# Gated graph layers: GRU tile updates spread over successive steps, and 10 instead of 12 of every 26 edge quads summed densely

## The reference

```
h = relu(layernorm(x)) @ lin_w.T + lin_b
for i in range(3):
    m = h @ weight[i]
    agg = segment_sum(m[src], dst, num_segments=12500)
    h = gru_cell(agg, h, w_ih, w_hh, b_ih, b_hh)
return x + h
# gru_cell: r = sigmoid(ir + hr); z = sigmoid(iz + hz)
#           n = tanh(inn + r * hn); h = (1 - z) * n + z * h
```

## Time and profile before

| what | value |
|---|---|
| median of 3 runs | 5887.51 us (5881.04 to 5918.47) |
| the profiled execution's own time | 5864.06 us |
| its span, first to last instruction | 5862.2 us |
| granted TensorE clock over the span | 0.787 of full speed |
| busy: PE / DVE / ACT / POOL | 65% / 31% / 19% / 59% |
| moved by DMA | 992.59 MB, 169 GB/s |

### The profile page before, as it was taken

One profiled execution on the slowest core, in us unless ns is written; L12 is line 12 of the kernel. 1 busy time (PEld: TensorE's weight loads), 2 busy tenths in 40 slices (PEclk: granted clock), 3 DMA queues, 4 the chain that ended last, 5 costly groups with the idle time before them and its releaser, 6 DMA issues.

```text
span 5862.2 us, 83667 instructions
## 1 busy us (share of the span) xinstructions
PE 3831.5 (65%) x31796; PEld 2541.3 (43%) x31797; DVE 1824.9 (31%) x7602; ACT 1102.4 (19%) x2163; POOL 3481.9 (59%) x3518
## 2 busy tenths in 40 slices
PE   4255555544455554444358888888875888888887
PEld 3144444433344444333224444544542444444454
DVE  7233434433333443333212222222221222222222
ACT  3133333333333333332100000000010000000000
POOL 5766555666665565665556566565645655656554
PEclk8566666766666666666679999999987999999998
DMA  5545444544445454444546666666664666666664
GB/s 181 153 128 141 139 136 138 148 128 130 135 131 143 140 146 126 137 135 118 171 150 213 204 204 212 209 206 204 217 211 150 211 202 200 210 206 199 204 214 140
DMA packets 726236, 992.59 MB, mean 169 GB/s; under 512 B 74424, under 2 KB 606520, under 8 KB 725816
## 3 DMA queue, kind: packets, MB, share of 16 engines
q1 hardware_dynamic: 471336, 582.73, 30.8%
q0 software_dynamic: 165888, 339.96, 21.2%
q10 hardware_dynamic: 88592, 64.25, 3.6%
HBM read 755.57 MB, written 231.08 MB: 168 GB/s over the span
## 4 chain that ended last, share of the span: by engine, by line
PE 52%; another core or an unknown queue 20%; issue 15%; ACT 5%; DVE 5%; DMA 1%; DVEq 1%; POOL 0%; ACTq 0%; POOLq 0%; SPq 0%
PE psum L758 26%; PE psum L738 9%; PE psum L736 4%; ACT pieces_region L591 4%; PE psum L716 4%; PE psum L704 3%; PE psum L675 1%; PE psum L676 1%; PE psum L677 1%; DVE onehot L1036 1%; DVE pieces_region L1137 1%; PE psum L688 1%; DVE aggT L1073 1%; DVEq L1026 1%
## 5 line engine op out<-in xcount | busy, mean ns | idle before, releaser
L468 POOL DMA_INDIRECT ring_region<-messages,edge_src x3456 | 3421.4, 990 | 2268.5 <-issue 1003.1
L758 PE MATMUL psum<-stage_region,pieces_region 128*128 128x432 f16 x9408 | 1862.7, 353 | 163.4 <-issue 161.6
L738 PE MATMUL psum<-pieces_region,stage_region 128*128 128x112 bf16 (+1 forms) x5376 | 998.4, 268 | 1160.3 <-ACT pieces_region L591 568.8
L758 PEld LDWEIGHTS psum<-stage_region,pieces_region 128*128 128x128 bf16 x9408 | 911.6, 99 | 1039.4 <-issue 317.2
L738 PEld LDWEIGHTS psum<-pieces_region,stage_region 128*128 128x128 bf16 x5376 | 641.0, 121 | 1345.2 <-issue 1266.0
L591 ACT CAST pieces_region<-psum 128x504 f16<-128x504 f32 x1344 | 759.5, 580 | 1830.8 <-remote 1005.8
L1059 DVE TENSOR_TENSOR aggT<-aggT,psum 128x36 f32 x864 | 166.7, 193 | 2741.8 <-remote 1658.7
L736 PE MATMUL psum<-pieces_region,stage_region 128*128 128x112 bf16 (+2 forms) x4032 | 837.8, 276 | 40.6 <-issue 40.4
L716 PE MATMUL psum<-onehot,ring_region 128*128 128x36 bf16 x10368 | 416.0, 184 | 454.4 <-issue 364.9
L716 PEld LDWEIGHTS psum<-onehot,ring_region 128*128 128x128 bf16 x10368 | 367.8, 101 | 537.8 <-issue 463.5
L1036 DVE TENSOR_SCALAR onehot<-iota_block,edge_rel 128x36 bf16<-128x36 bf16 x3456 | 531.1, 252 | 3.2 <-issue 2.9
(11 more groups left out here) (93 smaller groups left out, 1507.3 us busy)
## 6 DMA issues: line engine op xcount, KB each, us to landing
stage_region<-counts SPq DMA_DIRECT2D x448, 768.0 KB
counts<-pieces_region SPq DMA_DIRECT2D x192, 896.0 KB
ring_region<-messages,edge_src POOLq DMA_INDIRECT x3456
pieces_region<-messages SPq DMA_DIRECT2D x21, 1344.0 KB
temps<-states ACTq DMA_DIRECT2D x147, 128.0 KB
messages<-pieces_out ACTq DMA_DIRECT2D x98, 192.0 KB
states<-temps ACTq DMA_DIRECT2D x98, 128.0 KB
messages<-ring_region SPq DMA_DIRECT2D x25, 384.0 KB, 2.9
```

The costliest lines, as they stand in the source:

```text
L468: nc.gpsimd.indirect_dma_start(out=rows[:, n % RING, h * QC + c, :], out_offset=None, in_=messages[layer], in_offset=bass.IndirectOffsetOn ...
L738: mm = nc.tensor.matmul(by_block[:, :, covered:high], blocks_oh[j % 2][:, c, :], x_round[:, :, covered - low:], start=(c == 0), stop=True, ...
L758: mm = nc.tensor.matmul(psum[:, 6 + kg % 2, 0:DQ * W], res[:, b, piece * P:(piece + 1) * P], stage[v % ABUF][:, :, cols], start=(b == 0 an ...
```

## The change

Three things are changed.

`DQ` goes from 12 to 10. Layers 1 and 2 gather 16 quads of each superblock, so they have 8 steps a superblock and 128 steps a layer. 1,120 counting rounds stand in layer 0 in place of 1,344 (5.9 a step), and a dense matmul has 360 columns in place of 432; a layer still has 4,704 of them, now 12.6 blocks a step. A load of counts is 640 KB in place of 768 KB.

A tile update is divided over steps. In the step of the tile: state and gate products, r and z, the pre-activation. One step later: tanh, the clearing of the sums, the blend. Two steps later: the next messages, their pieces and, in layers 1 and 2, the store; in layer 0 the third piece and the store come three steps later. In layer 0 two tiles are at least two steps apart (`TILE_SPACING`). Steps that run past the last gather hold only tile phases.

In layer 0 all casts of a step come behind the gates in ACT's list, and DVE makes the pre-activation at the end of its step. In all layers DVE makes the one-hots ahead of the tile phases.

```
-DQ = 12
+DQ = 10
+TILE_SPACING = (2, 1, 1)
+LOW_LAG = (3, 2, 2)
...
+    def all_steps(layer, tiles_at):
+        return range(max(tiles_at) + 1 + LOW_LAG[layer])
...  ACT
+            def step_begin(layer, tiles_at, s):
+                if s - 1 in tiles_at:
+                    candidate(layer, tiles_at[s - 1])
+                if s - 2 in tiles_at:
+                    top_piece(layer, tiles_at[s - 2])
+                if s in tiles_at:
+                    gates(layer, tiles_at[s])
+
+            def step_end(layer, tiles_at, s):
+                if s - 2 in tiles_at:
+                    middle_piece(layer, tiles_at[s - 2])
+                if s - LOW_LAG[layer] in tiles_at:
+                    store(layer, tiles_at[s - LOW_LAG[layer]])
...
+                for s in all_steps(0, tiles_at):
+                    step_begin(0, tiles_at, s)
+                    if s < STEPS[0]:
+                        for r in range(rounds_by(s), rounds_by(s + 1)):
+                            evacuate(r)
+                    step_end(0, tiles_at, s)
...  PE
+                for s in all_steps(layer, tiles_at):
+                    n = STEP0[layer] + s
+                    if s < STEPS[layer]:
+                        rows_ready(n)
+                        for i in range(2 * QC):
+                            sum_chunk(n, i)
+                    if s - 2 in tiles_at:
+                        next_messages(layer, tiles_at[s - 2])
+                    if s in tiles_at:
+                        gate_products(layer, tiles_at[s], s)
...  DVE
+            def tile_phases(layer, tiles_at, s):
+                if s - 1 in tiles_at:
+                    blend_state(layer, layer * NT + tiles_at[s - 1])
+                if s - 3 in tiles_at and LOW_LAG[layer] == 3:
+                    low_piece(layer, tiles_at[s - 3])
+                if s - 2 in tiles_at:
+                    first_rest(layer, tiles_at[s - 2])
+                if s - 2 in tiles_at and LOW_LAG[layer] == 2:
+                    low_piece(layer, tiles_at[s - 2])
...
+                    tile_phases(layer, tiles_at, s)
...
+                    if s in tiles_at:
+                        gate_n(layer * NT + tiles_at[s])
```

More of the change, by code:

```diff
@@ L113, in schedule @@
             s = max(ready_after(layer, t) + 1, free)
-            at.setdefault(min(s, STEPS[layer]), []).append(t)
-            free = s + 1
+            at[s] = t
+            free = s + TILE_SPACING[layer]
         return at
     TILES_AT = [schedule(layer) for layer in range(LAYERS)]
-    TILES_LAST = [{STEPS[layer]: list(range(NT))} for layer in range(LAYERS)]
+    TILES_LAST = [{STEPS[layer] + TILE_SPACING[layer] * t: t for t in range(NT)} for layer in range(LAYERS)]
+    def all_steps(layer, tiles_at):
+        return range(max(tiles_at) + 1 + LOW_LAG[layer])
     def added(layer, s):
@@ L519, in state_tile_in, with gates @@
                 act.dma_start(hbuf[g % 2], states[:, t * TN:(t + 1) * TN]).then_inc(s_hl[g % 2], 16)
-            def tile_begin(layer, t):
+            def gates(layer, t):
                 g = layer * NT + t
-                last = layer == LAYERS - 1
-                if last:
-                    act.wait_ge(s_left, g)
-                    act.dma_start(blocks(xres), tile_rows(x, t * TN)).then_inc(s_xres, 16)
                 act.wait_ge(s_gate, 3 * g + 1)
@@ L617, in _ @@
             act.end_ifs()
-            finish(0)
             for layer in range(1, LAYERS):
-                for t in range(NT):
-                    tile_update(layer, t)
-                finish(layer)
+                state_tile_in(layer * NT)
+                for s in all_steps(layer, TILES_AT[layer]):
+                    step_begin(layer, TILES_AT[layer], s)
+                    step_end(layer, TILES_AT[layer], s)
             act.wait_ge(s_outst, 16 * NT)
@@ L825, in _ @@
                 pe.end_ifs()
-                next_messages(layer, NT - 1)
         @block.vector
@@ L1162, in layer_steps @@
                         dve.wait_ge(s_xiota, -(-XIOTA // RW))
-                    for t in tiles_at.get(s, ()):
-                        tile_update(layer, t)
-                    if n + 2 < TOTAL:
+                    if s < STEPS[layer] and n + 2 < TOTAL:
                         later = layer if s + 2 < STEPS[layer] else layer + 1
                         make_onehot(later, n + 2 - STEP0[later], n + 2)
-                    if layer == 0:
+                    tile_phases(layer, tiles_at, s)
+                    if layer == 0 and s < STEPS[0]:
                         for j in range(quads_by(s + 1), quads_by(s + 2)):
@@ L1174, in layer_steps @@
                                 add_superblock(layer, k, s)
-                for t in tiles_at.get(STEPS[layer], ()):
-                    tile_update(layer, t)
+                    if s in tiles_at:
+                        gate_n(layer * NT + tiles_at[s])
             for layer in range(LAYERS):
```

79 lines of the change are left out of this document (21 added, 58 removed).

## The result

The changed kernel takes 6099.15 us in the median (6092.27 to 6107.67, 4 runs), the kernel before 5895.35 us (5881.04 to 5918.47, 4 runs): 1.034 times as long, with a 95% interval of 1.030 to 1.038. The forecast was 6107 us. The profiled executions took 6101.52 and 5864.06 us, 237.5 us apart. Ratios with an interval compare runs in the faster of two states in which a program can run, and one run in the slower state, of the last experiment (5218.49 us), is left out of its ratio.

The account below looks back on a forecast made before the run. Bound: PE's stream and signals are held while POOL gathers back to back, so a step is a block plus about 2.7 us pause. Terms +400 - 20 - 140 - 17 - 10 + 30 = +243 on 5864 give 6107 us; range 5760 to 6270.

Parts of the forecast that it names:

- +400 for 32 steps: Layers 1 and 2: 16 more gathered steps each, at 12.5 us for a block of gathers plus a pause, +400 us.
- -20: Layers 1 and 2: narrower dense matmuls win a third of the mean pause above the usual one, -20 us, bounds 0 and -282.
- -17: Superblock adds: 10 for 12, 32 times, 64 x 0.26 us, -17 us, bounds 0 and -17.
- +30: TensorE's clock: the change makes PE idler; 0.9 us a superblock allowed, +30 us, bounds 0 and +300.
- the third rival: Layers 1 and 2: the clock falls for good, 98 tile steps take 3 us more each, 6371 us; chance 0.08.
- Ends of layers: Layer ends: PE's last three or four steps run without POOL, about 1.3 us shorter each, -10 us on the path.
- Layer 0: Layer 0: divided tile update and fewer counting rounds win two thirds of 203 us of stalls and slow gathers, -140 us.
- where I had 20: Layer 0, slow gathers beside DVE's dense one-hots: a sixth of those one-hots goes, -20 us, within the -140.
- where I had 120: Layer 0, POOL's waits behind tile updates: 120 us of the -140, from dividing the update and slack after stalls.
- the second rival: Layer 0 leaves the lock as PE delivers sums before signals are held: 11 us a step, 5751 us; chance 0.11.
- my mark of 12 us for being wrong on layer 0: Layer 0: the prediction would be wrong there if its step fell below 12 us.
- fewer rounds alone win nothing: Layer 0: 224 counting rounds fewer win nothing alone, as stall-free steps already last 12.41 us; they give slack after a stall.

Follow-up runs that it names:

- the last experiment: Kernel after with DVE's layer 0 pre-activation back ahead of the one-hots, on another chip: 4963.01 us, 1.043 of the kernel before; one slower run of 5218.49 us left out.

## Why the prediction was right

**The mechanism.** Steps are counted, not matmuls: that carried the forecast's sign, and the experiments bear it out where the lock is present. Without POOL's gathers the hold is gone, a stop moves the pause, and a fifth of the columns shortens the step by 0.16 us alone. The prediction's sentence, that PE is held while POOL issues back to back, is too coarse: its own row of 72 matmuls in 10 us lies beside 8 gathers without a pause, and the counts above say that 55 to 87 matmuls get through behind a pause before PE creeps. What I also left unsaid is that the lock isn't a matter of the kernel alone: on one chip it was absent.

**The steps' terms**, +400 for 32 steps, -20, -17 and +30: +393 forecast. Measured: layer 1 went from 112 x 12.57 to 128 x 12.38 us, layer 2 from 112 x 12.58 to 128 x 12.40, +178 and +178, together +356. The mis-sized one is the length of the step, 12.39 and not 12.5 us and more. Of the 0.19 us, 0.11 are POOL's shorter waits (2.60 to 2.49) and 0.06 its gathers (856.25/896 = 0.956 to 970.81/1024 = 0.948 us, eight times). For the +30 for the clock no run shows a cost. The clock fell, from 0.91 to 0.84, but the step became shorter all the same. It did not fall for good and tile steps did not spill over, so the third rival did not come; what it would cost at full width wasn't tested. How much the -20 and the -17 gave by themselves no run tells.

The rule of the Trainium skill on this ("TensorE: Matmul & The Clock Gate", section "HAM oscillation — how this bites in real kernels"), that gaps put the array back on the low clock, agrees with the fall from 0.91 to 0.84. No run here shows that it cost time.

**Ends of layers**, -10 forecast. The wait before layer 2 fell from 58.6 to 51.5 us, and the time after the last gathers of layer 2 from 44.1 (5862.2 - 5818.1) to 31.5 us (6099.7 - 6068.2): -20.

**Layer 0**, -140 forecast, -99 measured, and of other parts than I said. POOL's gathers took 1654.74 in place of 1713.71 us: -59, where I had 20. What it waited for in layer 0, in the kernel before and in the kernel after:

```profile
POOL ring_region L468 <- PE psum L716: 380.8, 62, 13.6
POOL ring_region L468 <- remote: 203.1, 89, 4.2
```

```profile
POOL ring_region L473 <- PE psum L712: 295.6, 55, 7.9
POOL ring_region L473 <- remote: 254.1, 108, 4.4
```

583.9 us before and 549.7 after: -34, where I had 120. The wait at the layer's end gave 2 and the gaps of issue 4. I read this so: the stalls that I saw behind a tile update were mostly the lock itself, which dividing the update doesn't remove; I had counted everything above 12.41 us a step as curable. No run tests that reading by itself. Layer 0's steps are still 12.9 us, so the second rival did not come, and my mark of 12 us for being wrong on layer 0 wasn't reached.

The first two experiments, run together on one chip, say which half does what in layer 0. With the divided updates alone the gathers take 1653.88 us, as in the kernel after, though the one-hots of twelve quads in each superblock are made; with ten dense quads alone they take 1760.50 us. So the 59 us come from the divided updates, DVE's new order included, and the -20 that I gave for a sixth fewer one-hots has nothing behind it. With the waits it is the other way round: 518.1 us with the divided updates alone, 438.0 us with ten dense quads alone. I had said that fewer rounds alone win nothing.

The slow gathers stand beside the 1176-column one-hots of DVE; 127 of 141 us above 0.945 us a gather lie there before, 68 of 82 after, summed over the 1,664 gathers of layer 0. Timelines of DVE and POOL of the kernel after, the one-hots and two gathers beside them:

```profile
1512.82 2.46 DVE L1127 TENSOR_SCALAR pieces_region<-pieces_region,stage_region 128x1176 bf16<-128x1176 f16 x4
```

```profile
1512.09 0.95 POOL L473 DMA_INDIRECT ring_region<-messages,edge_src  x1 [0.30 <-issue]
1513.34 0.94 POOL L473 DMA_INDIRECT ring_region<-messages,edge_src  x1 [0.30 <-issue]
```

Here the gathers keep their 0.94 us and DVE pays, 2.46 us for the four in place of 2.21. The prediction used half of the rule of the Trainium skill ("SBUF — State Buffer", section "SBUF: two separate sides"), that VectorE locks GpSimd out. The page also says that whichever of the two starts first gets the ports and the other waits. The first of these gathers agrees: it began at 1512.09, ahead of the one-hots. The second does not: it began at 1513.34, behind the first two one-hots (1512.82 and 1513.28), and kept its time too. So the order of starts isn't the whole of it. That the new order on DVE brings the gather first more often was argued, and the last experiment doesn't settle it.

**The sum.** Forecast +393 - 10 - 140 = +243, measured +356 - 20 - 99 = +237, which is the difference of the two executions. The result is closer than its parts, and that is luck: the steps came out 37 us below the forecast, the ends of layers 10 us below, layer 0's gain 41 us short of it, and the errors cancelled.

**What the profile was to show.** Layers of about 1600 us: 1636 and 1619. Layer 0 between 2600 and 2720: 2716, at the edge. PE below 80% busy: 72% and 71%. Dense matmuls 0.153 us apart: 0.153 in the median. Steps of 12.3 to 12.8 us: 12.38 and 12.40. Pauses of 2.5 to 2.8 us in most steps: only in 63 of 127; 22 boundaries have none and 22 have more than 3.2 us. The mean is steady, the single pause is not.

## What to carry to other kernels

When stages with different work have steps of the same length, look for what the steps have in common, and price a change by that. Read a late signal by the row of the engine that waits for it, not by the end of the one that sends it: sums begun at 3638.5 and added at 3643.4 were the whole case. Before cutting an engine's work, ask whether the same move adds work to the engine whose issuing sets the pace, and run the kernel before on more than one chip before believing that a pause belongs to the kernel. A stop that only moves a pause where PE is idle need not be free where PE is busy.

## What the runs showed of the hardware that I had not expected

- Under unbroken indirect gathers PE starts 55 to 87 matmuls behind a pause, whatever their width, and then one only every 0.7 to 2.8 us: 4 in 10 us, at a DMA share of 0.30. Nearly the same program on another chip: 60 in 10 us. The kernel before took 5777 to 5895 us where this hold was seen and 4762 us where it was not. What differs, and which part of PE's path is held, no run tells.
- A pause of POOL of some 2.5 to 3 us, at a block's end or in its middle, lets the stream go on. Stops under 1.2 us, with a gather still under way, were followed by 4.6 us at the next boundary.
- Beside plain transfers issued by SP at 271 GB/s PE was busy 93% of the time.
